# Column sums of a quantised context on four column tiles of the array side by side, in a gated cross-attention block

## What is computed

```python
def fake_quant(x, scale, zp):            # QMIN 0, QMAX 255
    q = jnp.clip(jnp.round(x / s + z), QMIN, QMAX)
    return (q - z) * s
# step 1: a quantised product with the context (2 batches of 2048 x 2048)
x = x + tanh(g_xattn[0]) * matmul(fake_quant(layernorm(x), s1, z1), fake_quant(ctx, s2, z2))
# step 2: a low-rank product, rank 512
weight = U * S[None, :] @ V.T
x = x + tanh(g_ffn[0]) * einsum('bti,oi->bto', layernorm(x), weight)
```

## Time and profile before

| what | value |
|---|---|
| time, median of 3 runs | 652.93 us (645.51 to 656.64) |
| the profiled execution | 650.33 us |
| its span, first to last instruction | 648.5 us |
| granted TensorE clock, mean | 0.981 |
| PE busy | 595.3 us (92%), 2709 matmuls recorded |
| DVE, ACT, POOL busy | 384.1 (59%), 210.7 (32%), 162.4 us (25%) |
| column sums, line 433 | 125 matmuls recorded of 128 |
| column corrections, line 672 | 8, 0.765 us each in the middle |

### The profile page before, as it was taken

One profiled execution on the slowest core, in us unless ns is written; L12 is line 12 of the kernel. 1 busy time (PEld: TensorE's weight loads), 2 busy tenths in 40 slices (PEclk: granted clock), 3 DMA queues, 4 the chain that ended last, 5 costly groups with the idle time before them and its releaser, 6 DMA issues.

```text
span 648.5 us, 7357 instructions
## 1 busy us (share of the span) xinstructions
PE 595.3 (92%) x2709; PEld 267.5 (41%) x2740; DVE 384.1 (59%) x714; ACT 210.7 (32%) x254; POOL 162.4 (25%) x123
## 2 busy tenths in 40 slices
PE   2698998899999798997499999999999999999997
PEld 1343443344444343443144444444444444444443
DVE  6849779894394837473334667564747373745212
ACT  5897785813040304064435221030303030211000
POOL 1369650003050500631112570021120404040000
PEclk9899999999999989998699999999999999999999
DMA  8999936548647283399989414236281809080522
GB/s 289 387 386 386 295 90 142 101 126 195 201 124 185 65 201 85 64 293 273 233 211 305 149 35 93 54 68 177 46 192 25 209 17 209 35 178 1 128 68 97
DMA packets 151011, 104.03 MB, mean 160 GB/s; under 512 B 113984, under 2 KB 113984, under 8 KB 150976
## 3 DMA queue, kind: packets, MB, share of 16 engines
q1 hardware_dynamic: 141984, 86.27, 51.0%
q10 hardware_dynamic: 8992, 17.30, 8.9%
HBM read 58.99 MB, written 16.78 MB: 117 GB/s over the span
## 4 chain that ended last, share of the span: by engine, by line
PE 49%; DMA 17%; DVE 15%; ACT 7%; SPq 6%; issue 5%; POOL 0%; ACTq 0%; DVEq 0%; POOLq 0%
PE bank L458 19%; DMA out_dram<-ring 5%; PE bank L485 5%; PE bank L486 5%; PE bank L487 5%; PE bank L506 5%; PE bank L508 5%; PE bank L507 5%; DMA stage<-in_ctx_dram 4%; ACT u8r L596 4%; DMA xT<-xs 3%; DVE xs L983 2%; SPq L288 2%; DMA ring<-in_x_dram 2%; DVE u_hl L1040 2%
## 5 line engine op out<-in xcount | busy, mean ns | idle before, releaser
L458 PE MATMUL bank<-q,qT 128*128 128x512 bf16 x872 | 199.1, 381 | 3.5 <-DMA qT<-qn 2.2
L458 PEld LDWEIGHTS bank<-q,qT 128*128 128x128 bf16 x896 | 88.1, 99 | 109.7 <-issue 3.5
L485 PE MATMUL bank<-v_hl,xT 128*128 128x512 f16 x256 | 97.8, 382 | 12.1 <-DMA xT<-xs 9.8
L220 POOL TENSOR_SCALAR ring<-ring,bvec 128x2048 f32<-128x2048 f32 x16 | 32.9, 2058 | 301.6 <-DVE bvec L920 301.6
L506 PE MATMUL bank<-u_hl,hbuf 128*128 128x512 f16 x240 | 92.5, 385 | 12.4 <-DVE ring L998 6.4
L486 PE MATMUL bank<-v_hl,xT 128*128 128x512 f16 x256 | 97.8, 382 | 0.0
L487 PE MATMUL bank<-v_hl,xT 128*128 128x512 f16 x256 | 97.6, 381 | 0.0
L508 PE MATMUL bank<-u_hl,hbuf 128*128 128x512 f16 x240 | 92.3, 384 | 0.0
L507 PE MATMUL bank<-u_hl,hbuf 128*128 128x512 f16 x240 | 92.2, 384 | 0.0
L225 POOL TENSOR_TENSOR ring<-ring,corr 128x512 f32<-128x512 f32 x64 | 87.2, 1393 | 7.8 <-ACT corr L672 6.7
L945 DVE SCALAR_TENSOR_TENSOR ring<-bank,const,ring 128x512 f32<-128x512 f32 x64 | 47.7, 745 | 68.7 <-PE bank L458 66.4
(11 more groups left out here) (110 smaller groups left out, 517.4 us busy)
## 6 DMA issues: line engine op xcount, KB each, us to landing
out_dram<-ring SPq DMA_DIRECT2D x64, 256.0 KB, 3.7
ring<-in_x_dram SPq DMA_DIRECT2D x62, 256.0 KB, 4.0
v_hl<-in_ctx_dram SPq DMA_DIRECT2D x26, 512.0 KB, 11.3
stage<-in_ctx_dram ACTq DMA_DIRECT2D x18, 512.0 KB, 6.1
q<-in_ctx_dram ACTq DMA_DIRECT2D x14, 512.0 KB, 7.4
u_hl<-in_L_ffn_V_dram SPq DMA_DIRECT2D x8, 512.0 KB, 11.6
stage<-in_ctx_dram SPq DMA_DIRECT2D x6, 512.0 KB, 11.4
stage<-in_L_ffn_U_dram SPq DMA_DIRECT2D x2, 512.0 KB, 4.3
```

What stands on the lines that cost most here:

```text
L458: mm = nc.tensor.matmul(unit_bank(t, n)[:, :], qT_of(t)[:, k, :], q2[:, n, k, :], start=(k == 0), stop=(k == KT - 1))
L485: nc.tensor.matmul(h_bank(u)[:, :], hi, v_hl[:, k, 0, :], start=first, stop=False)
```

## The change

A column sum uses only 32 columns of ones at a time: k-tile k goes to column tile k % 4 of the array and to the 32 rows of the bank that belong to it, so that four k-tiles can be in the array side by side. Each group of 32 rows then holds a partial sum over four k-tiles. ACT scales the bank by 1/32 into `corr` (`column_parts`), PE adds the 128 rows with one f32 product with a matrix of ones (`colsum_total`), back into the same bank, and ACT applies the correction as before (`column_correction`), which now waits for that product. In batch 0, for n of 1 to 3, PE takes two chunks at a time. The new steps are put into the orders of PE and ACT by hand, and some column corrections move.

```diff
             def colsum(b, n, k0=0, k1=KT):
...
-                    mm = nc.tensor.matmul(colsum_bank(b, n)[:, :], ones_b[:, :], q2[:, n, k, :],
-                                          start=(k == 0), stop=(k == KT - 1))
+                    g = k % CG * GW
+                    mm = nc.tensor.matmul(colsum_bank(b, n)[g:g + GW, :], ones_b[:, g:g + GW], q2[:, n, k, :],
+                                          start=(k < CG), stop=(k >= KT - CG), tile_position=(0, g))
                 if k1 == KT:
                     mm.then_inc(colsum_done, 1)
+
+            def colsum_total(b, n):
+                pe.wait_ge(parts_ready, NQ * b + n + 1)
+                nc.tensor.matmul(colsum_bank(b, n)[:, :], ones_f[:, :], corr[:, n * W:(n + 1) * W],
+                                 start=True, stop=True).then_inc(colsum_summed, 1)
...
             for n in range(1, NQ):
-                for i in range(CQ):
-                    colsum(0, n, CK * i, CK * i + CK)
+                for i in range(0, CQ, 2):
+                    colsum(0, n, CK * i, CK * i + 2 * CK)
                     for t in range(G if n < NQ - 1 else 1):
-                        s1_part(t, n, CK * i, CK * i + CK)
+                        s1_part(t, n, CK * i, CK * i + 2 * CK)
+                    if i == 2:
+                        colsum_total(0, n - 1)
             s1_part(1, NQ - 1)
+            colsum_total(0, NQ - 1)
             s1_part(2, NQ - 1)
...
             for n in range(NQ - 1):
                 colsum(1, n)
+                if n > 0:
+                    colsum_total(1, n - 1)
             mm4(7)
+            colsum_total(1, NQ - 2)
             colsum(1, NQ - 1)
-            s1(8)
+            s1_part(8, 0)
+            colsum_total(1, NQ - 1)
+            for n in range(1, NQ):
+                s1_part(8, n)
...
-            def column_correction(b, n):
+            def column_parts(b, n):
                 act.wait_ge(colsum_done, NQ * b + n + 1)
                 if b > 0:
                     act.wait_ge(x1_pre, unit(TB * b - 1, n) + 1)
-                elif n == 0:
-                    act.wait_ge(const_ready, 1)
                 elif n == NQ - 1:
                     act.wait_ge(smax_ready, 1)
+                nc.scalar.activation(corr[:, n * W:(n + 1) * W], colsum_bank(b, n)[:, :], ACT.Copy,
+                                     scale=1.0 / GW).then_inc(parts_ready, 1)
+
+            def column_correction(b, n):
+                act.wait_ge(colsum_summed, NQ * b + n + 1)
+                if b == 0 and n == 0:
+                    act.wait_ge(const_ready, 1)
...
             for c in range(8, 14):
                 op1(c)
+            column_parts(0, 0)
+            for c in range(14, 19):
+                op1(c)
             column_correction(0, 0)
-            for c in range(14, 20):
-                op1(c)
+            op1(19)
             root1(3)
             op2(3)
             for c in range(20, 24):
                 op1(c)
-            column_correction(0, 1)
+            column_parts(0, 1)
             op1(24)
             op1(25)
             v_square(VORD[0])
             op1(26)
             op1(28)
+            column_correction(0, 1)
+            op1(29)
+            column_parts(0, 2)
+            op1(30)
+            v_square(VORD[1])
+            v_square(VORD[2])
             column_correction(0, 2)
-            v_square(VORD[1])
-            op1(29)
-            op1(30)
-            for j in VORD[2:5]:
-                v_square(j)
+            v_square(VORD[3])
+            v_square(VORD[4])
+            column_parts(0, 3)
+            v_square(VORD[5])
             column_correction(0, 3)
-            for j in VORD[5:8]:
-                v_square(j)
+            v_square(VORD[6])
+            v_square(VORD[7])
             u_squares(2)
...
-            stream(22, 30)
+            stream(22, 29)
+            column_parts(1, 0)
+            stream(29, 30)
             root1(9)
+            column_parts(1, 1)
+            column_correction(1, 0)
             op2(9)
+            column_parts(1, 2)
+            column_correction(1, 1)
             stream(30, 32)
-            for n in range(NQ):
-                column_correction(1, n)
+            column_correction(1, 2)
+            column_parts(1, 3)
+            column_correction(1, 3)
             root1(10)
```

More of the change, by code:

```diff
@@ L28, in gated_block_program @@
     NST = 10
+    CG = 4
+    GW = P // CG
     NU8 = 8
@@ L132, in gated_block_program @@
         colsum_done = sem("colsum_done")
+        parts_ready = sem("parts_ready")
+        colsum_summed = sem("colsum_summed")
         corr_ready = sem("corr_ready")
```

## The result

The changed kernel takes 668.85 us (median of four runs, 668.58 to 668.98), the kernel before 653.09 in the same session (645.51 to 656.64): ratio 1.0281, interval 1.0195 to 1.0366. The profiled execution took 668.58 (span 666.8), 18.3 us more than the profiled one of before. The forecast was 662.8 with a range of its own of 658 to 667, so it was 6 us short; 668.85 lies in the wide range of 651 to 673. (Ratios leave out runs over 1.5% above the fastest of their program.) That it falls on the 668.8 of rival (a) is chance: the profile shows nothing of that rival's mechanism.

A forecast was written before the change was run, and what follows sets the result against it. It took the supply of chunks, not TensorE, to bound the column-sum stretches; 11.2 us in batch 0 plus 1.3 in batch 1, 12.5 on the profiled 650.33, gave 662.8 us; own range 658 to 667, wide range 651 to 673.

The forecast's parts named there:

- rival (a): TensorE's array empties at shape changes and the tiles go in turn: 668.8 us, slower by more than 2%; chance 0.20.
- The hold: Batch 0: ACT's column_correction(0,1) behind op1(28) delays POOL, DVE and TensorE; u_squares(0) and mm3(0) 11.2 us later.
- The prices: On TensorE, a round of four tiles costs 0.4 us (0.216 to 1.19), an f32 product 0.86 (0.43 to 1.73).
- The slow start after the hole: Batch 0: after PE idles until chunk 25 at 78.2 us, matmuls start 0.42 us apart at 1.2 GHz; 2.4 GHz saves 1.1.
- Rival (b): Later waits pay back batch 0's delay: 11 us there at 122 us, not at 300; 652 us in all; chance 0.17.
- Rival (c): TensorE was the bound all along: 12.9 us saved, 637.4 us, faster by about 2%; chance 0.07.
- the term for batch 1: Batch 1's column sums, around mm4(7) and unit (8,0): rounds save 2.4 us, products and slips take it; +1.3 us.
- After 122 us all is chained to that: Everything after batch 0's context shifts by the same 11.2 us as mm3(0).

The follow-up runs named there:

- e1: Kernel before with one line moved: ACT's column_correction(0,1) behind op1(28), no tiles or products; 661.29 us, ratio 1.0118.
- e2: Changed kernel with products (0,1) and (0,2) earlier on TensorE, and ACT's steps for them moved along; 657.05 us, ratio 1.0089.
- e11: Changed kernel with column_correction(0,1) one place earlier on ACT, ahead of op1(28); 665.28 us, ratio 1.0219.
- e3: Kernel before with tiles, products and ACT's new order in batch 1 only; 651.98 us, ratio 1.0006.
- e5: Changed kernel with products (0,1) and (0,2) early in batch 0, and batch 1 as in the kernel before; 656.25 us, ratio 1.0071.
- e9: Kernel before with the change's batch 0 part only, same program as e4, measured again with more rounds; 663.43 us, ratio 1.0200.
- e4: Kernel before with tiles, products and ACT's new order in batch 0 only; 662.62 us, ratio 1.0158.
- e6: Changed kernel, unaltered, measured again beside the kernel before; 669.45 us, ratio 1.0286.
- e7: Changed kernel with batch 1's products behind mm4(7) and ACT's activations for them behind the last chunk; 669.97 us, ratio 1.0270.
- e8: Changed kernel with SP's transpose of h for row tile 7 issued ahead of a load of x; 667.14 us, ratio 1.0230.
- e10: Kernel before with column_correction(0,1) behind op1(28) and batch 1's part of the change; batch 0 without tiles or products; 662.94 us, ratio 1.0191.

## Why the prediction fell short, point by point

**The hold, step by step, was right.** corr(0,1) was forecast ready at 69.9 and was at 69.29 + 0.76 = 70.05; POOL's wait 10.6 and 10.83; its pre done 73.9 and 73.92; its last op2 78.8 and 78.29; chunk 31 82.2 and 82.52; PE's next full pair 78.2 and 78.90; product (0,3) done 89.7 and 90.62; u_squares(0) 95.7 and 96.39; v_low(0) done 108.6 and 109.27; mm3(0) +11.2 and +11.85. e1, e2 and e11 show the cause by putting it in alone, taking it out, and shrinking it. Batch 0's part as a whole, 10.3 and 13.0 us, brackets the 11.2.

**The prices were right.** A round was put at 0.4 between 0.216 and 1.19, and took 0.43. A product was put at 0.86 between 0.43 and 1.73, and took 0.86 to 0.95. The slow start after the hole came as in the earlier trace rows: from 78.90 on matmuls ran at half rate to about 82 (granted 0.50 from 78.9 to 82.0).

**Rival (a) falls** though its time fits. In the row of 32 at 352.72 the four tiles of a round start within 0.01 us of each other, and the next round follows after 0.216, so they don't go in turn. The change of shape does cost: 0.43 for a round between full matmuls against 0.216 in a row of tiles, so 0.21 us for the way in and out. The Trainium skill ("TensorEngine Tiling (Array Packing)", Tiling Modes, Key Properties) says that a change of mode drains TensorE; the trace agrees in kind, at less than the 0.33 that two empty-outs would take.

**Rival (b) is not borne out.** Its sign was that the delay is gone at 300 us. In the table below it is still 10.0 us at row tile 7 (332 us before) both in the changed kernel and in e1. e1's ratio of 7.7 us leaves room for a part paid back in other executions, no more. **Rival (c) falls**: e3 and e5 relieve TensorE with no hold or a small one, and neither is faster than before.

**The step that failed is the term for batch 1, +1.3 us, and with it the sentence "After 122 us all is chained to that".** The term was worked out for a batch 1 merely shifted by 11 us. With little or no shift it holds: e3 came out 1.3 us early there, 1.0006 in time, and e2 costs about what e5 does. On top of the delay from batch 0 it was another matter. Against e9 the whole takes 1.0286 instead of 1.0200, about 5.6 us more; the intervals overlap at their ends. With both measurements of either program the excess is clearer: the two ratios of the changed kernel and the two of batch 0's part (e4, e9), each pair weighted by its intervals, differ by 6.6 us, with an interval of about 3 to 10, and the plain means of ten runs each, 669.0 and 663.9, by 5.2. So there is an excess of some 5 us, and its size is rough.

Where it comes in is harder to see. The table has the shift against before of ACT's first step behind mm3(u), the split of its result (us, one profiled execution each):

```
row tile u             0     2     3     5     7     8 (batch 1)
batch 1 with tiles, delayed
changed             11.8  11.8  13.7  15.4  10.0  18.3
e6 changed again    12.8  12.8  14.7  15.0  12.6  12.3
e7 other order      11.7  11.7  14.3  15.1  14.9  23.8
e8 h earlier        13.4  13.4  15.7  16.2  16.8  18.9
e10 hold, batch 1   11.2  11.2  10.9  11.3   8.8  11.7
e11 one line         9.5   9.5  11.5  12.9  15.1  15.2
batch 1 with full sums, delayed
e9 batch 0 alone    12.3  12.3  13.9  14.5  14.0  12.4
e4 the same         12.2  12.2  14.6  15.7  17.5  17.7
e1 hold alone       11.0  11.0  11.3  10.9  10.0  13.9
little or no delay
e3 batch 1 alone     1.0   1.0   1.7   1.7  -0.6  -0.8
e2 products early    2.7   2.7   5.0   4.2   2.6   2.5
e5 e2's batch 0      2.8   2.8   3.8   5.6   6.3   5.1
```

In the first profile 8.3 us are added between row tiles 7 and 8, where the column sums of batch 1 are. But e6 and e11, with tiles, add nothing there, e1, with full sums, adds 3.9, and e4, with full sums, is 17.7 late at the end, as late as the changed kernel. So single profiles do not tell tiles from full sums; they show only how the loss comes about where it does. PE's timeline of e9 is the contrast, with full matmuls in the same place (L520 is mm4):

```profile
356.75 10.31 PE L438 MATMUL bank<-q,ones_b 128*128 128x512 bf16 x47
366.90 0.38 PE L520 MATMUL bank<-u_hl,hbuf 128*128 128x512 f16 x1
```

and its window:

```profile
371.00:375.00 4.00, 4.00 (x20) 1.86 (x19) 3.67 (x7) 1.06 (x2) 3.92 (x3) 1.00 0.20 48
```

Full sums take 10.3 us, and while they run the chunks and h arrive, so mm4(7) follows without a wait at 366.90. With tiles the sums are done at once and PE waits for the same arrivals: in all eight profiles with tiles the matmuls of chunk 23 start 9.7 to 14.2 us after the last one of mm4(6). e6, which began its sums 1.5 us sooner than e9, starts mm4(7) at 366.94, no earlier. So the time that the tiles save in batch 1 ahead of mm4(7) turns into waiting. And the waiting can lower the clock: in the first profile mm4(7) begins with 13 matmuls in 5.50 us (370.26 to 375.76) instead of 2.81, **2.7 us that the prediction did not have**; it had charged a low clock only in batch 0.

Full sums do not always cover the arrivals. In e1 chunk 23 came later, PE waited for it, and mm4(7) ran at the low clock too, as PE's timeline and a window of e1 show:

```profile
366.32 0.61 PE L433 MATMUL bank<-q,ones_b 128*128 128x512 bf16 x2 [3.75 <-DVE q L935]
```

```profile
367.00:371.00 4.00, 4.00 (x12) 1.49 (x11) 1.85 (x4) 3.52 (x5) 2.05 (x2) 0.57 0.88 256
```

In the delayed kernels with tiles the lowest granted clock in a 4-us window of mm4(7) was 0.50 in the changed kernel and in e7, e8 and e10, 0.59 in e11 and 1.00 in e6. With full sums it was 1.00 in e9 and e4 and 0.57 in e1. So the low clock goes with the waiting, and tiles make that longer; they are not its only cause. That the rest of the excess is the later arrival of chunk 23 and h is argued from the waits, not shown by a run.

**What stays open.** It is open why those transfers came later in one execution of the changed kernel than in another (chunk by chunk they queue with stores and loads of x; e8 moved one and another wait took over). The 2 us that the table adds at row tile 3 in most kernels with batch 0's tiles are ACT's own, which has two chunks to do just ahead: PE's mm3(3) and mm3(4) are still 11.8 late in the changed kernel. On PE the extra appears in mm4(3), in a wait of 7.31 us for a y unit (4.33 before); why DVE is late there is open too. Runs of one kernel spread by up to 11 us, and two profiles of one program end 5 to 6 us apart (the changed kernel and e6, e4 and e9), so a single shift in this table past row tile 2 is uncertain by several us.

## What to carry to other kernels

Before a step is cut in two and handed back and forth between engines that work in order, look at what each half now stands behind: here the one line `column_correction(0, 1)`, moved behind a chunk that had yet to arrive, held POOL, then DVE, then TensorE, and made the next stage 11 us late where the step itself costs under 1. Work taken from an engine in a stretch where the supply ends last is no gain, and on TensorE it can be a loss, because the waiting that replaces it can lower the clock for the work that follows (2.7 us in the first profile). A sum over parts should be checked with the delay of the first part put in: a stage that cost nothing on time cost some 5 us when it came late.

No version tried was faster than the kernel before; e3 equals it, and the best with batch 0's tiles, e5, is 0.7% slower.

## What the hardware showed beyond expectation

- Four 32-column tiles side by side do 32 matmuls of 512 columns in 1.91 us: the four of a round start within 0.01 us of each other (352.717 to 352.727), and rounds follow at 0.216 us, the interval of single full matmuls, so the rate is four times theirs.
- Alternating with full matmuls costs 0.21 us a round on top (0.43 instead of 0.216), as much again as the round.
- An f32 product of 128x128 by 512 columns takes 0.86 to 0.95 us, two matmul instructions, four times a bf16 matmul's 0.216; in the slow stretch it took 2.01 (361.42 to 363.43).
- After 6.80, 1.31 and 2.19 us of waiting with little work in between, TensorE ran at 1.2 GHz (granted 0.50) through 5.5 us of unbroken matmuls.
